# The rounded operand of the cross attention, made in the tokens' layout and transposed as bf16

## The chip, the cores and the metric

The kernel runs on one core of a Trainium2 chip. A core has five engines that run side by side and meet at semaphores: TensorE (PE in the profile, with its weight loads shown apart as PEld), VectorE (DVE), ScalarE (ACT), GpSimd (POOL) and SyncE (SP), which issues most of the DMAs. Work goes through the on-chip memory SBUF; TensorE writes into eight banks of PSUM. The metric is the device time of one execution in microseconds (us), here the median of three runs.

## The reference

One decoder layer on 4 batches of 512 tokens with 512 features. Three blocks, each behind its residual and followed by a layer normalisation without parameters: an attention-like mixer (`x1` is what comes out of it), a product with the context whose two operands are rounded to FP8, and an MLP with eight chosen experts for each token. Only the second block is touched by the change, together with the first units of the MLP that run beside it:

```python
def _fp8_quant_dequant(x):
    scale = 448.0 / jnp.maximum(jnp.max(jnp.abs(x)), 1e-12)
    q = jnp.clip(x * scale, -448.0, 448.0).astype(jnp.float8_e4m3fn)
    return q.astype(jnp.float32) / scale
out = jnp.einsum('bmk,bkn->bmn', _fp8_quant_dequant(x1), _fp8_quant_dequant(ctx_2048)) + mask
x2 = _layernorm(x1 + out)
mlp = silu(x2 @ gate_w) * (x2 @ up_w) @ down_w          # and the experts' sum is added
out = _layernorm(x2 + mlp + experts)
```

## The kernel before

A first phase computes `x1` for all four batches and leaves it in `xall`, 16 tiles of 128 tokens by 512 features, tokens along the partitions. The change lies in the start of the second phase (from line 1090; from about 212 us on).

**Rounding.** A tile of `x1` goes through four instructions. ScalarE scales it by `scale_x` into `y_q[i]` (L1420) and multiplies its magnitude by a constant into `m_q[i]` (L1422); VectorE adds and subtracts a number that size (L1547, L1549 in `quantise`), which leaves the value rounded to four bits, stored as bf16 in `x_q`. The product with the context (`cross`, L1879) needs features along the partitions, so TensorE first transposes the f32 tile with four 128x128 transposes (`transposes`, L1871) into a bank `gu`, and ScalarE's scaling reads that bank. All the rounding thus happens on transposed data, and `x_q` feeds `cross` directly.

**The units.** The MLP runs in units `n`: for one batch and 256 of the 2048 inner features, `gate_up` makes for each half `c` a gate product and an up product (12 matmuls 128x512 each, since every f32 operand is split into a high and a low part), ScalarE applies silu (`silu`, L1441), VectorE multiplies (`middle`, L1605), ScalarE and GpSimd split the result (`high_h` L1447, `low_h` L1302), and `down` or `down_early` multiplies it back into the banks `ob` (L1942 to L1946). Units 0 to 2 are interleaved with the second block: in unit `n` TensorE runs gate and up of half 0, then `cross(n + 1)`, then half 1, `down_early(n, 0)`, the transposes of the finished `x2` of batch n+1 (`x2_transposes`, L1862) and `down_early(n, 1)`. The transposes of `x1` for batch n+2 stand in units 0 and 1 in two groups of eight, one ahead of gate of half 1 and one between its gate and its up. Those of batch 1 stand at the very start, between the four tiles of `cross(0)`.

**VectorE beside it.** In unit `n` its queue holds `middle(n, 0)`, the residual of batch n+1 with its statistics (`residual`, L1557 and L1559), the variance (L1566), `quantise` of tile 0 of batch n+2, the normalisation (L1588), `middle(n, 1)`, `quantise` of tile 1, the low part of `x2` (L1594), two tiles of `accumulate` (L1614), `quantise` of tile 2, two more of `accumulate`, and `quantise` of tile 3. Every engine runs its queue strictly in this written order.

**GpSimd beside it.** It adds the mask to a batch of `xall` with a DMA that accumulates (`add_mask`, L152). That DMA changes `xall`, so it waits until the transposes of that batch have read it (`x1t_mm`). Behind it in the queue stands `power` (L1308), the inverse square root that the normalisation waits for, and then `low_h`.

Of the kernel before, what the change touches and what calls it, by code (L numbers as in the profile page):

```python
# [16 lines left out]
BF16 = mybir.dt.bfloat16  # L17
# [72 lines left out]
def decoder_layer(nc, x, ctx, mask, w_in, b_in, w_out, b_out, gamma, beta, w_q, keys, down_embed, up_embed,  # L90
# [14 lines left out]
    with ExitStack() as whole:  # L105
# [57 lines left out]
        with ExitStack() as first:  # L163
# [126 lines left out]
            def _(pool):  # L290
# [72 lines left out]
                add_mask(0)  # L363
# [726 lines left out]
        with ExitStack() as second:  # L1090
# [13 lines left out]
            junk2 = sb("junk2", [P, D], BF16)  # L1104
            key_sb = sb("key_sb", [P, 2, 2, NK], F32)
# [20 lines left out]
            late_junk = sb("late_junk", [P, D], BF16)  # L1126
# [32 lines left out]
            minus_first, squared = sem("minus_first"), sem("squared")  # L1159
            minus_done, squared_late, shift_done, y_act = sem("minus_done"), sem("squared_late"), sem("shift_done"), sem("y_act")  # L1160
# [5 lines left out]

            def x1t_bank(b, i):

                return i if b < 2 else i % 2

# [119 lines left out]
            def _(pool):  # L1290
# [42 lines left out]
                add_mask(1)  # L1333
# [66 lines left out]
            def _(act):  # L1400
# [12 lines left out]
                def scaled(b, tiles):  # L1413
                    for i in tiles:

                        j = TB * b + i
                        act.wait_ge(x1t_mm, j + 1)
                        if j >= TB:
                            act.wait_ge(q_done, j - TB + 1)
# [41 lines left out]
                scaled(0, range(TB))  # L1461
                scaled(1, (0, 1))
                for i in range(TB):
                    deviation(i)
                for n in range(TB - 1):
                    high_x2(n)
                    if n == 0:
                        scaled(1, (2, 3))
                        high_w(2, 0, 0, 2, 0)
                        high_w(3, 0, 0, 3, 1)  # L1470
                    unit(n, 0)
                    if n + 2 < TB:
                        scaled(n + 2, (0, 1))
                    silu(n, 1)
                    if n + 2 < TB:
                        scaled(n + 2, (2, 3))
# [58 lines left out]
            def _(dve):  # L1535
# [3 lines left out]
                def quantise(b, tiles):  # L1539
                    for i in tiles:  # L1540
# [309 lines left out]
            def _(pe):  # L1850
# [14 lines left out]
                def transposes(b, tiles, bank, count, free):  # L1865

                    for i in tiles:
                        free(i)
                        for c in range(KC):
                            j = TB * b + i  # L1870
                            last = nc.tensor.transpose(gu[bank(i)][:, c * P:(c + 1) * P], xall[:, j * D + c * P:j * D + (c + 1) * P], ident[:])  # L1871
                        last.then_inc(count, 1)
# [9 lines left out]
                def gate_up(n, g_set, tb, c, w_loads, between=None, up_free=None):  # L1882
# [5 lines left out]
                    if n < TB - 1 and c == 0:  # L1888
# [4 lines left out]
                        else:  # L1893
                            pe.wait_ge(y_done, TB + 2)
# [61 lines left out]
                def own_bank(i):  # L1956
                    return i

                def x1_bank(b):
                    return lambda i: x1t_bank(b, i)  # L1960

                def first_half_free(n):
                    return lambda i: pe.wait_ge(mid_done, GC * n + 1)
# [99 lines left out]
```

## Time and profile before

| | |
|---|---|
| median of 3 runs | 798.92 us (798.86 to 799.06) |
| the profiled execution's own time | 799.09 us |
| its span, first to last instruction | 797.2 us |
| TensorE busy | 778.9 us, 98% of the span |
| VectorE busy | 669.1 us, 84% |
| GpSimd busy | 368.5 us, 46% |
| ScalarE busy | 320.3 us, 40% |

A busy time is the sum over the records of an engine. Matmuls overlap in their pipeline: a 128x512 matmul is recorded as 0.39 us long, and the next one starts about 0.23 us behind it, so costs on TensorE are read from start to start. "[0.39 <-POOL h_lo L1302]" behind a row of the timeline means that the engine stood idle for 0.39 us ahead of it and that this instruction ended the wait. Some matmul records are missing from a trace, so that a row x15 can stand for 16.

### The profile page before, as it was taken

The numbers are of one execution on the slowest core, as the hardware profiler recorded it, in microseconds if no ns is written. First come the engines' busy times: TensorE is split into PE (matmuls) and PEld (weight loads), VectorE is DVE, ScalarE is ACT, GpSimd is POOL, SyncE is SP. The second block draws the span as 40 slices with busy tenths as digits, with TensorE's granted clock in tenths as the row PEclk, the third lists the DMA queues.
The fourth block names the chain that finished last, engine by engine and source line by source line (L and its number), as shares of the span: only waits on it lengthen the run. The fifth ranks groups of instructions, "written<-read, shape, count | busy, mean of one in ns | idle before, by whom it ended". The sixth has DMA issues, their size and how long they took to land. (4 is left out here: it accounts for less than half of the span.)

```text
span 797.2 us, 10711 instructions
## 1 busy us (share of the span) xinstructions
PE 778.9 (98%) x3610; PEld 639.3 (80%) x3614; DVE 669.1 (84%) x1330; ACT 320.3 (40%) x704; POOL 368.5 (46%) x305
## 2 busy tenths in 40 slices
PE   8999999999899999999999999999999999999996
PEld 7888888888667878888888888888877877878785
DVE  6887679898889870566699999999999999999997
ACT  6444337366574412232534323334233333333324
POOL 1331222233123411024467767676766667766433
PEclk9999999999999999999999999999999999999999
DMA  8667505625454538001222322322333233232113
GB/s 317 237 143 175 106 2 127 162 80 91 84 132 119 146 104 266 1 1 34 69 59 84 91 80 73 95 78 58 95 94 95 90 93 112 64 91 68 44 53 158
DMA packets 51046, 81.16 MB, mean 102 GB/s; under 512 B 17487, under 2 KB 26447, under 8 KB 50480
## 3 DMA queue, kind: packets, MB, share of 16 engines
q0 software_dynamic: 24240, 32.96, 19.4%
q1 hardware_dynamic: 25168, 47.52, 17.1%
q8 instruction: 28, 0.46, 0.2%
q10 hardware_dynamic: 1584, 0.01, 0.1%
q14 instruction: 26, 0.21, 0.1%
HBM read 110.44 MB, written 12.58 MB: 154 GB/s over the span
## 5 line engine op out<-in xcount | busy, mean ns | idle before, releaser
L1852 PE MATMUL gu<-x_hi,w_hi 128*128 128x512 f32 x516 | 202.1, 392 | 1.9 <-ACT mid L1441 1.9
L1854 PE MATMUL gu<-x_hi,w_lo 128*128 128x512 f32 x516 | 200.9, 389 | 0.0
L1853 PE MATMUL gu<-x_lo,w_hi 128*128 128x512 f32 x516 | 200.8, 389 | 0.0
L1302 POOL TENSOR_TENSOR h_lo<-mid,h_hi 128x512 fp32r<-128x512 f32 x62 | 80.6, 1320 | 103.5 <-ACT h_hi L1447 103.0
L1457 ACT ACTIVATE gates<-dots 128x1 f32<-128x1 f32 x144 | 29.2, 203 | 232.4 <-DVE dots L1696 226.4
L1852 PEld LDWEIGHTS gu<-x_hi,w_hi 128*128 128x128 f32 x516 | 96.9, 188 | 24.3 <-ACT mid L1441 4.4
L1854 PEld LDWEIGHTS gu<-x_hi,w_lo 128*128 128x128 f32 x516 | 96.8, 188 | 20.3
L1853 PEld LDWEIGHTS gu<-x_lo,w_hi 128*128 128x128 f32 x516 | 96.9, 188 | 19.8
L1321 POOL DMA_INDIRECT ctx_q<-table_dram,row_i x64 | 80.4, 1257 | 62.2 <-DVE xall L1705 42.5
L1321 POOL DMA_INDIRECT scratch<-table_dram,row_i x64 | 82.5, 1289 | 39.8 <-issue 23.6
L1605 DVE TENSOR_TENSOR mid<-gu,mid 128x512 f32<-128x512 f32 x64 | 44.2, 690 | 62.3 <-PE gu L1854 41.1
L1926 PE MATMUL ob<-w_lo,h_hi 128*128 128x512 f32 x224 | 87.2, 389 | 0.0
L1925 PE MATMUL ob<-w_hi,h_hi 128*128 128x512 f32 x224 | 87.2, 389 | 0.0
L1696 DVE CUSTOM_DVE_ANT_0 junk<-x_tok,scratch 128x512 bf16<-128x512 f32 x64 | 80.5, 1257 | 0.3
L1930 PE MATMUL ob<-w_hi,h_lo 128*128 128x512 f32 x224 | 69.2, 390 | 0.8 <-POOL h_lo L1302 0.8
L1696 DVE CUSTOM_DVE_ANT_0 junk<-x_tok,ctx_q 128x512 bf16<-128x512 f32 x64 | 66.0, 1032 | 0.5
L1297 POOL TENSOR_TENSOR w_lo<-xhat,w_hi 128x1024 fp32r<-128x1024 f32 x21 | 50.7, 2415 | 23.8 <-ACT w_hi L1411 15.9
L1768 DVE TENSOR_TENSOR xall<-ob,xall 128x512 f32<-128x512 f32 x95 | 59.6, 683 | 2.3 <-PE ob L1930 0.3
L1447 ACT ACTIVATE h_hi<-mid 128x512 fp32r<-128x512 f32 x62 | 36.0, 620 | 58.3 <-PE ob L1930 31.8
L1441 ACT ACTIVATE mid<-gu 128x512 f32<-128x512 f32 x64 | 37.2, 583 | 42.2 <-PE gu L1854 33.6
L1930 PEld LDWEIGHTS ob<-w_hi,h_lo 128*128 128x128 f32 x224 | 41.8, 188 | 10.2 <-POOL h_lo L1302 1.6
L1925 PEld LDWEIGHTS ob<-w_hi,h_hi 128*128 128x128 f32 x224 | 42.0, 188 | 8.8
(258 smaller groups left out, 1449.9 us busy)
## 6 DMA issues: line engine op xcount, KB each, us to landing
stage<-in_ctx SPq DMA_DIRECT2D x7, 1024.0 KB, 6.0
total<-prod POOLq DMA_DIRECT2D x11, 512.0 KB, 4.7
xall<-half_bo POOLq DMA_DIRECT2D x4, 1024.0 KB, 9.9
xhat<-in_L_ffn_gate_w SPq DMA_DIRECT2D x8, 512.0 KB
xhat<-in_L_ffn_up_w SPq DMA_DIRECT2D x8, 512.0 KB
xall<-in_mask_Bx1xS_ff POOLq DMA_DIRECT2D x4, 1024.0 KB, 10.5
xhat<-in_L_ffn_down_w SPq DMA_DIRECT2D x8, 512.0 KB
x_dram<-xall SPq DMA_DIRECT2D x4, 1024.0 KB, 7.0
```

Of the source, the lines that this page charges most:

```text
L1297: nc.gpsimd.tensor_tensor(flat(lo, r), stage_of(r, slot), flat(hi, r).bitcast(F32), ALU.subtract).then_inc(wlo_done, 1)
L1302: nc.gpsimd.tensor_tensor(lo[:, c], mid[c][:], hi[:, c].bitcast(F32), ALU.subtract).then_inc(hlo_done, 1)
L1321: nc.gpsimd.indirect_dma_start(rows[k], None, table_dram[:, :], bass.IndirectOffsetOnAxis(ap=row_i[t % 2][:, k:k + 1], axis=0), bounds_che ...
L1605: nc.vector.tensor_tensor(mid[c][:], gu[2 * c + 1][:], mid[c][:], ALU.mult).then_inc(mid_done, 1)
L1696: nc.vector.tensor_tensor_reduce(out=junk2[:], in0=x2_tok[par][:], in1=row[:, 0:D], scale=1.0, scalar=0.0, op0=ALU.mult, op1=ALU.add, accu ...
L1768: nc.vector.tensor_tensor(tile(j), ob[i][:], tile(j), ALU.add).then_inc(acc_done, 1)
L1852: nc.tensor.matmul(dst, lhs[0], rhs[0], start=start, stop=False)
L1853: nc.tensor.matmul(dst, lhs[0], rhs[1], start=False, stop=False)
L1854: return nc.tensor.matmul(dst, lhs[1], rhs[0], start=False, stop=stop)
L1925: nc.tensor.matmul(ob[i][:], h[0][:, c, ts], w_high[:, c], start=(c == 0), stop=False)
L1926: nc.tensor.matmul(ob[i][:], h[0][:, c, ts], w_low[:, c], start=False, stop=False)
L1930: last = nc.tensor.matmul(ob[i][:], h[1][:, c, ts], w_high[:, c], start=False, stop=(c == GC - 1))
```

## The change

For batches 1 to 3 the rounding works on `xall` itself, in the tokens' layout. ScalarE's scaling reads the tile in SBUF, `quantise` writes the rounded tile as bf16 into new tiles `x_qt[i]`, TensorE transposes those (`xq_transposes`, with a bf16 identity that GpSimd makes) into the banks `ob`, read as bf16, and ScalarE copies each bank to `x_q` (`copy_xq`). `cross` then waits for the copies. Batch 0 stays as it was. The sixteen transposes of a batch now stand in unit 0 behind up of half 0, and in units 1 and 2 between gate and up of half 0. ScalarE's instructions of a batch are grouped: four scalings at once and, after the silu of half 1, four magnitudes at once. `add_mask` of batches 1 to 3 waits for the scalings. At the start, where batch 1 was transposed, five transposes of the identity stand ahead of each of tiles 1 to 3.

```diff
@@ add_mask
-        def add_mask(b):
-            nc.gpsimd.wait_ge(x1t_mm, TB * (b + 1))
+        def add_mask(b, read, count):
+            nc.gpsimd.wait_ge(read, count)
@@ GpSimd
                 nc.gpsimd.memset(key_sb[:], 0.0).then_inc(key_zero, 1)
+                nc.gpsimd.tensor_copy(ident_b[:], ident[:]).then_inc(ident_b_done, 1)
...
-                        add_mask(n + 2)
+                        add_mask(n + 2, y_scaled, TB * (n + 3))
@@ ScalarE
-                def scaled(b, tiles):
...
-                        nc.scalar.activation(y_q[i], gu[x1t_bank(b, i)][:], ACT.Copy, scale=scale_x[:, 0:1]).then_inc(y_scaled, 1)
-                        act.wait_ge(y_scaled, j + 1)
-                        nc.scalar.activation(m_q[i], y_q[i], ACT.Abs, scale=ROUND_TO_4_BITS).then_inc(y_done, 1)
+                def scaled(b, i):
+                    j = TB * b + i
+                    if b:
+                        act.wait_ge(q_done, j - TB + 1)
+                    else:
                         act.wait_ge(x1t_mm, j + 1)
+                    nc.scalar.activation(y_q[i], tile(j) if b else gu[i][:], ACT.Copy, scale=scale_x[:, 0:1]).then_inc(y_scaled, 1)
+
+                def magnitude(b, i):
+                    j = TB * b + i
+                    act.wait_ge(y_scaled, j + 1)
+                    nc.scalar.activation(m_q[i], y_q[i], ACT.Abs, scale=ROUND_TO_4_BITS).then_inc(y_done, 1)
+
+                def copy_xq(b):
+                    for i in range(TB):
+                        act.wait_ge(xq_mm, TB * (b - 1) + i + 1)
+                        if i == 0:
+                            act.wait_ge(cross_mm, TB * b)
+                        nc.scalar.activation(x_q[:, i].rearrange("p c n -> p (c n)"), ob[i][:].bitcast(BF16)[:, 0:D], ACT.Copy).then_inc(xq_done, 1)
@@ VectorE, quantise
-                        if b and i == 0:
-                            dve.wait_ge(cross_mm, TB * b)
+                        if b > 1:
+                            dve.wait_ge(xq_mm, j - 2 * TB + 1)
...
-                        nc.vector.scalar_tensor_tensor(x_q[:, i].rearrange("p c n -> p (c n)"), m, ROUND_SUBNORMAL, y, ALU.max, ALU.subtract).then_inc(q_done, 1)
+                        nc.vector.scalar_tensor_tensor(x_qt[i][:] if b else x_q[:, i].rearrange("p c n -> p (c n)"), m, ROUND_SUBNORMAL, y, ALU.max, ALU.subtract).then_inc(q_done, 1)
@@ TensorE
+                def xq_transposes(b, free):
+                    for i in range(TB):
                         free(i)
+                        pe.wait_ge(q_done, TB * b + i + 1)
                         for c in range(KC):
+                            last = nc.tensor.transpose(ob[i][:].bitcast(BF16)[:, c * P:(c + 1) * P], x_qt[i][:, c * P:(c + 1) * P], ident_b[:])
+                        last.then_inc(xq_mm, 1)
...
                 def cross(b, free, tiles=range(TB)):
                     for i in tiles:
                         free(i)
-                        pe.wait_ge(q_done, TB * b + i + 1)
+                        if b:
+                            pe.wait_ge(xq_done, TB * (b - 1) + i + 1)
+                        else:
+                            pe.wait_ge(q_done, i + 1)
...
                 for n in range(TB - 1):
-                    gate_up(n, 0, n, 0, 2 if n == 0 else None)
-                    cross(n + 1, freed(acc_done, TB * (n - 1)) if n else nothing)
-                    if n + 2 < TB:
-                        transposes(n + 2, (0, 1), x1_bank(n + 2), x1t_mm, first_half_free(n))
-                        gate_up(n, 0, n, 1, None, lambda: transposes(n + 2, (2, 3), x1_bank(n + 2), x1t_mm, freed(y_done, TB * (n + 2) - 2)))
-                    else:
-                        gate_up(n, 0, n, 1, None)
+                    def next_xq():
+                        xq_transposes(n + 1, freed(acc_done, TB * (n - 1)) if n else nothing)
+                    gate_up(n, 0, n, 0, 2 if n == 0 else None, next_xq if n else None)
+                    if n == 0:
+                        next_xq()
+                    cross(n + 1, nothing)
+                    gate_up(n, 0, n, 1, None)
                     down_early(n, 0, freed(z2_done, TB * n))
                     x2_transposes(n + 1, x2_bank_free(n))
                     down_early(n, 1, nothing)
```

On TensorE in unit 1, at the end of gate of half 0, with bank numbers: before, the first products of up follow the last of gate.

```order
L1900 MATMUL gu0<-x2_lo,w_hi 128x512 [waits l2_done]
L1900 MATMUL gu0<-x2_lo,w_hi 128x512 x3
L1852 MATMUL gu1<-x2_hi,w_hi 128x512
L1853 MATMUL gu1<-x2_lo,w_hi 128x512
L1854 MATMUL gu1<-x2_hi,w_lo 128x512
```

Now the sixteen transposes of batch 2 stand there, each tile behind its `q_done`.

```order
L1919 MATMUL gu0<-x2_lo,w_hi 128x512 [waits l2_done]
L1919 MATMUL gu0<-x2_lo,w_hi 128x512 x3
L1889 MATMUL ob0<-ident_b,x_qt0 128x128 [waits q_done,acc_done]
L1889 MATMUL ob0<-ident_b,x_qt0 128x128 x3
L1889 MATMUL ob1<-ident_b,x_qt1 128x128 [waits q_done,acc_done]
L1889 MATMUL ob1<-ident_b,x_qt1 128x128 x3
L1889 MATMUL ob2<-ident_b,x_qt2 128x128 [waits q_done,acc_done]
L1889 MATMUL ob2<-ident_b,x_qt2 128x128 x3
L1889 MATMUL ob3<-ident_b,x_qt3 128x128 [waits q_done,acc_done]
L1889 MATMUL ob3<-ident_b,x_qt3 128x128 x3
L1870 MATMUL gu1<-x2_hi,w_hi 128x512
```

The transposes moved from either side of gate of half 1 to the front of up of half 0, and took with them a wait for the rounded tiles.

On ScalarE in unit 1, before: silu and high part of half 0, and the eight instructions of batch 3 around the silu of half 1 (L1420 scales, L1422 takes the magnitude).

```order
L1441 ACTIVATE mid0<-gu0 128x512 [waits hlo_done,gate_mm]
L1447 ACTIVATE h_hi<-mid0 128x512 [waits down_mm,mid_done]
L1420 ACTIVATE scratch<-gu0,scale_x 128x512 [waits q_done,x1t_mm]
L1422 ACTIVATE scratch<-scratch 128x512 [waits y_scaled]
L1420 ACTIVATE scratch<-gu1,scale_x 128x512 [waits q_done,x1t_mm]
L1422 ACTIVATE scratch<-scratch 128x512 [waits y_scaled]
L1441 ACTIVATE mid1<-gu2 128x512 [waits hlo_done,gate_mm]
L1420 ACTIVATE scratch<-gu0,scale_x 128x512 [waits q_done,x1t_mm]
L1422 ACTIVATE x2_tok0<-scratch 128x512 [waits y_scaled]
```

The same place now (L1432 is the copy of `copy_xq`, L1425 the magnitude).

```order
L1451 ACTIVATE mid0<-gu0 128x512 [waits hlo_done,gate_mm]
L1432 ACTIVATE scratch<-ob0 128x512 [waits cross_mm,xq_mm]
L1432 ACTIVATE scratch<-ob1 128x512 [waits xq_mm]
L1432 ACTIVATE scratch<-ob2 128x512 [waits xq_mm]
L1432 ACTIVATE scratch<-ob3 128x512 [waits xq_mm]
L1457 ACTIVATE h_hi<-mid0 128x512 [waits down_mm,mid_done]
L1420 ACTIVATE scratch<-xall,scale_x 128x512 [waits q_done] x4
L1451 ACTIVATE mid1<-gu2 128x512 [waits hlo_done,gate_mm]
L1425 ACTIVATE scratch<-scratch 128x512 [waits y_scaled] x2
L1425 ACTIVATE x2_tok0<-scratch 128x512 [waits y_scaled] x2
```

Four copies came in between silu and high part of half 0, and all magnitudes of batch 3 moved behind the silu of half 1.

## Rows read from the trace of the kernel before

**Rows 1.** The page's first part: busy time, share of the span, instructions.
```profile
PE 778.9 (98%) x3610; PEld 639.3 (80%) x3614; DVE 669.1 (84%) x1330; ACT 320.3 (40%) x704; POOL 368.5 (46%) x305
```

**Rows 2.** Windows: busy us of each engine, then clock share, DMA share, GB/s.
```profile
280.00:300.00 20.00, 19.93 (x98) 15.40 (x98) 14.26 (x28) 4.01 (x8) 3.55 (x3) 1.00 0.41 118
300.00:340.00 40.00, 40.00 (x194) 33.74 (x193) 12.84 (x61) 10.24 (x18) 5.31 (x4) 1.00 0.39 126
600.00:700.00 100.00, 98.94 (x434) 80.72 (x433) 93.82 (x161) 36.27 (x109) 71.24 (x52) 1.00 0.33 95
```

**Rows 3.** Timeline of TensorE, unit 1: start, duration, what, idle before.
```profile
253.46 1.07 PE L1900 MATMUL gu<-x_lo,w_hi 128*128 128x512 f32 x4
254.37 0.39 PE L1852 MATMUL gu<-x_hi,w_hi 128*128 128x512 f32 x1
...
257.32 3.40 PE L1879 MATMUL ob<-ctx_q,scratch 128*128 128x512 bf16 x15
260.55 1.04 PE L1871 MATMUL gu<-ident,xall 128*128 128x128 f32 x8
261.35 0.47 PE L1852 MATMUL gu<-x_hi,w_hi 128*128 128x512 f32 x1
```

**Rows 4.** Groups by line: weight loads; busy us, mean ns | idle before.
```profile
L1879 PEld LDWEIGHTS ob<-ctx_q,scratch 128*128 128x128 bf16 x64 | 5.7, 98 | 8.1 <-DVE scratch L1549 1.1 <-issue 0.8
L1871 PEld LDWEIGHTS gu<-ident,xall 128*128 128x128 f32 x48 | 5.6, 140 | 1.4
```

**Rows 5.** Timeline of ScalarE: first deviation, copies out of PSUM, a magnitude, a silu.
```profile
220.14 0.72 ACT L1435 ACTIVATE junk<-xall,z_minus 128x512 bf16<-128x512 f32 x1 [0.21 <-DVE z_minus L1574]
...
248.25 2.04 ACT L1428 ACTIVATE x_hi<-gu 128x512 fp32r<-128x512 f32 x4
...
263.15 0.63 ACT L1422 ACTIVATE scratch<-scratch 128x512 bf16<-128x512 f32 x1
264.40 0.60 ACT L1441 ACTIVATE mid<-gu 128x512 f32<-128x512 f32 x1 [0.61 <-PE gu L1854]
```

**Rows 6.** Timeline of VectorE, unit 0: first residual and normalisation.
```profile
236.44 0.75 DVE L1557 SCALAR_TENSOR_TENSOR xall<-ob,unscale,xall 128x512 f32<-128x512 f32 x1 [0.98 <-DMA xall<-in_mask_Bx1xS_ff]
...
244.21 1.92 DVE L1588 TENSOR_SCALAR xall<-xall,mv,rstd 128x512 f32<-128x512 f32 x4 [0.20 <-POOL rstd L1308]
```

**Rows 7.** Timeline of TensorE, unit 0: its wait in `down_early(0, 1)`.
```profile
249.25 0.50 PE L1946 MATMUL ob<-w_hi,h_lo 128*128 128x512 f32 x1 [0.39 <-POOL h_lo L1302]
```

**Rows 8.** Timeline of VectorE: low part of x2, last rounding of batches 2 and 3.
```profile
248.86 2.48 DVE L1594 TENSOR_TENSOR x_lo<-gu,x_hi 128x512 fp32r<-128x512 f32 x4 [0.81 <-ACT x_hi L1428]
...
255.70 0.69 DVE L1549 SCALAR_TENSOR_TENSOR scratch<-x_tok,scratch 128x512 bf16<-128x512 bf16 x1
...
279.45 0.69 DVE L1549 SCALAR_TENSOR_TENSOR scratch<-x_tok,scratch 128x512 bf16<-128x512 bf16 x1
```

**Rows 9.** Timeline of VectorE, unit 1, from middle to the normalisation.
```profile
257.36 0.69 DVE L1605 TENSOR_TENSOR mid<-gu,mid 128x512 f32<-128x512 f32 x1 [0.36 <-PE gu L1854]
...
264.23 0.17 DVE L1566 TENSOR_SCALAR var<-mv 128x4 f32<-128x4 f32 x1
264.32 0.69 DVE L1547 SCALAR_TENSOR_TENSOR scratch<-scratch 128x512 f32<-128x512 bf16 x1
265.05 0.69 DVE L1549 SCALAR_TENSOR_TENSOR scratch<-scratch 128x512 bf16<-128x512 bf16 x1
267.97 1.92 DVE L1588 TENSOR_SCALAR xall<-xall,mv,rstd 128x512 f32<-128x512 f32 x4 [2.23 <-POOL rstd L1308]
```

**Rows 10.** Timeline of GpSimd, unit 1: the mask's DMA and the power.
```profile
265.54 1.33 POOL L152 DMA_DIRECT2D xall<-in_mask_Bx1xS_ff  x1 [4.87 <-PE gu L1871]
266.39 1.55 POOL L1308 TENSOR_TENSOR rstd<-var,neg_half 128x4 f32<-128x4 f32 x1
```

**Rows 11.** Timeline of TensorE, unit 2: first product of up, of gate of half 1.
```profile
278.14 0.39 PE L1852 MATMUL gu<-x_hi,w_hi 128*128 128x512 f32 x1
...
284.14 0.58 PE L1852 MATMUL gu<-x_hi,w_hi 128*128 128x512 f32 x1
```

More of the change, by code:

```diff
@@ L362, in _ @@
                 last_z_rstd(slice(0, TB))
-                add_mask(0)
+                add_mask(0, x1t_mm, TB)
                 for i in range(TB):
@@ L1104, in decoder_layer @@
             junk2 = sb("junk2", [P, D], BF16)
+            x_qt = [sb(f"x_qt{i}", [P, D], BF16) for i in range(TB)]
+            ident_b = sb("ident_b", [P, P], BF16)
             key_sb = sb("key_sb", [P, 2, 2, NK], F32)
@@ L1125, in decoder_layer @@
             late_square = sb("late_square", [P, TB + 1], F32)
-            late_junk = sb("late_junk", [P, D], BF16)
+            late_junk = x_qt[0]
             z_sum = sb("z_sum", [P, TB], F32)
@@ L1159, in decoder_layer @@
             minus_first, squared = sem("minus_first"), sem("squared")
+            ident_b_done, xq_mm, xq_done = sem("ident_b_done"), sem("xq_mm"), sem("xq_done")
             minus_done, squared_late, shift_done, y_act = sem("minus_done"), sem("squared_late"), sem("shift_done"), sem("y_act")
@@ L1165, in tile @@
                 return xall[:, bass.ds(j * D, D)]
-            def x1t_bank(b, i):
-                return i if b < 2 else i % 2
             def x2t_bank(b, i):
@@ L1330, in _ @@
                 nc.gpsimd.memset(key_sb[:], 0.0).then_inc(key_zero, 1)
+                nc.gpsimd.tensor_copy(ident_b[:], ident[:]).then_inc(ident_b_done, 1)
                 power_pair(0)
                 power_pair(1)
-                add_mask(1)
+                add_mask(1, y_scaled, 2 * TB)
                 for n in range(TB):
@@ L1459, in experts @@
                         nc.scalar.activation(coef[:, t % 2, k:k + 1], gates[:, t % 2, k:k + 1], ACT.Copy, scale=prob[:, t, k:k + 1]).then_inc(coef_done, 1)
-                scaled(0, range(TB))
-                scaled(1, (0, 1))
+                for i in range(TB):
+                    scaled(0, i)
+                    magnitude(0, i)
+                for i in range(TB):
+                    scaled(1, i)
                 for i in range(TB):
@@ L1467, in _ @@
                     if n == 0:
-                        scaled(1, (2, 3))
+                        for i in range(TB):
+                            magnitude(1, i)
                         high_w(2, 0, 0, 2, 0)
                         high_w(3, 0, 0, 3, 1)
-                    unit(n, 0)
+                    silu(n, 0)
+                    copy_xq(n + 1)
+                    high_h(n, 0)
                     if n + 2 < TB:
-                        scaled(n + 2, (0, 1))
+                        for i in range(TB):
+                            scaled(n + 2, i)
                     silu(n, 1)
                     if n + 2 < TB:
-                        scaled(n + 2, (2, 3))
+                        for i in range(TB):
+                            magnitude(n + 2, i)
                     high_h(n, 1)
@@ L1863, in x2_transposes @@
                         last.then_inc(x2t_mm, 1)
-                def transposes(b, tiles, bank, count, free):
-                    for i in tiles:
+                def xq_transposes(b, free):
+                    for i in range(TB):
                         free(i)
+                        pe.wait_ge(q_done, TB * b + i + 1)
                         for c in range(KC):
-                            j = TB * b + i
-                            last = nc.tensor.transpose(gu[bank(i)][:, c * P:(c + 1) * P], xall[:, j * D + c * P:j * D + (c + 1) * P], ident[:])
-                        last.then_inc(count, 1)
+                            last = nc.tensor.transpose(ob[i][:].bitcast(BF16)[:, c * P:(c + 1) * P], x_qt[i][:, c * P:(c + 1) * P], ident_b[:])
+                        last.then_inc(xq_mm, 1)
                 def cross(b, free, tiles=range(TB)):
@@ L1954, in nothing @@
                     pass
[L1956 to L1963, printed above, removed]
[L1965 to L1974 removed]
+                def x2_bank_free(n):
+                    return lambda i: pe.wait_ge(mid_done, GC * n + 1 + i // 2)
                 def keep_running(bank, count):
@@ L1983, in _ @@
                 keep_running(ob[3], 5)
-                for i in range(TB):
-                    transposes(1, (i,), own_bank, x1t_mm, freed(y_done, 0))
+                cross(0, nothing, (0,))
+                for i in range(1, TB):
+                    pe.wait_ge(y_done, i + 1)
+                    keep_running(gu[0], 5)
                     cross(0, nothing, (i,))
-                pe.wait_ge(y_done, TB + 2)
                 for i in range(1, TB):
```

15 lines of the change are left out of this document (1 added, 14 removed).

## The prediction, made before the changed kernel was run

> **What bounds the kernel now.** I read the page's shares first: TensorE is busy for 98% of the span [rows 1]. The windows say whether that holds at the place of the change: from 280 to 300 us it works 19.93 of 20 us, from 300 to 340 all of it, and from 600 to 700 us it idles for 1.06 [rows 2]. So what TensorE gets more to do, or waits longer for, in the first units moves all that comes behind. Its timeline gives the prices, from start to start. The up product of half 0 in unit 1 begins at 254.37, and the first recorded `cross` product, the second of 16, at 257.32; the first stood at 257.10, so 12 products take 2.73 us [rows 3]. `cross` runs from there to 260.55, 3.45 us, 0.216 each. Eight f32 transposes take 0.80 from start to start, and the product behind them is recorded 0.08 longer than the others, so 0.88, 0.11 each.
>
> **What is removed.** Units 0 and 1 lose two groups of eight f32 transposes each: 4 x 0.88 = 3.52 us of TensorE time in a stretch without slack. The sixteen of batch 1 at the start stood between waits for VectorE's rounding of batch 0, and fifteen transposes of the identity stand in their place: nothing.
>
> **What is added on TensorE.** 48 bf16 transposes, which no row shows. From below: a bf16 product of 512 columns takes 0.216, a quarter of that for 128 columns is 0.054. From above: the f32 transpose's 0.11. The bf16 weight load is recorded at 98 ns and that of the f32 transpose at 140 [rows 4]; I scale 0.11 by that, 0.08, so 1.28 us for a batch. By count alone the change comes out at 3.84 - 3.52 = +0.3 us, and between -0.9 and +1.8 at the two ends.
>
> The trace shows f32 transposes 0.11 us apart although each is recorded 0.27 long (eight in 1.04 us from the first start to the last end [rows 3]). The Trainium skill, "TensorE: Matmul & The Clock Gate", Part 4, puts a 128x128 bf16 transpose at about 275 ns in a kernel's context; if that were the step and not only the length, this sum would not hold, and the last rival below would be the forecast.
>
> **ScalarE's copies.** Four more instructions for each batch. The nearest row is the copy of `x2` out of PSUM, four in 2.04 us [rows 5], 0.51 each and 0.6 for a single one. In units 1 and 2 they lie beside the 2.73 us of up; in unit 0 the first lies open. The grouping costs ScalarE nothing in itself: in the start its fourth scaling of batch 1 follows the last rounding of batch 0 at once, and it idled for 0.21 before the first deviation at 220.14 [rows 5]. The small cast of the identity lies in GpSimd's idle start.
>
> **Unit 0.** TensorE finishes up, transposes tile 0 (0.32), waits for its copy (0.6 and two handovers of about 0.05) and starts `cross`; the other twelve transposes lie beside the copy for the most part. `cross` starts some 1.2 us later than before. Of half 1 both groups of transposes are gone, 1.76, so TensorE is 0.6 us early at the down products. That gain ends in a wait. The chain of VectorE in unit 0 begins with the landing of batch 1's mask at 236.44, whose DMA the change doesn't move, and leads over residual, variance and normalisation at 244.21 [rows 6] to `middle(0, 1)`, the high and the low part, and the product that waited for GpSimd until 249.25 [rows 7]. Only the 0.20 us for the power goes, since batch 2's mask is issued before the variance is there. I carry -0.18 us out of unit 0 (from -0.2 to +0.3).
>
> **Unit 1, where the new wait decides.** The fourth tile of batch 2 is rounded at 255.70 + 0.69 = 256.39 [rows 8]. VectorE works towards that without a gap from 248.86 on: the low part of `x2`, two accumulations, tile 2, two accumulations, tile 3. The change leaves this order. Before, that was in time, as `cross` needed the tile only at the end of up. Now its transposes stand ahead of up. TensorE comes to them at 254.37 - 0.18 + 12 x 0.08 = 255.15, the tile is there at 256.21: a wait of 1.06 us that nothing covers, since up stands behind it in the same queue. Up starts at 256.21 + 0.06 + 0.32 = 256.59 instead of 254.37, **+2.22 us**.
>
> What becomes of that: up (2.73) and `cross` (3.45) bring gate of half 1 to 262.77, against 261.35 [rows 3], +1.42, and without the second group TensorE is at the down products at +0.54. VectorE's middle at 257.36 and variance at 264.23 [rows 9] move by 2.22, to 266.45. But VectorE had waited 2.23 us for the power, which stood behind the mask's DMA, and that behind the transposes of tiles 2 and 3 for 4.87 us [rows 10]. Now the mask follows the four scalings, near 263.6, and the power follows the variance: 266.65 + 1.55 = 268.2. The rounding of batch 3's tile 0 stands ahead of the normalisation. It now waits for its magnitude, which stands behind silu: 264.40 + 1.42 + 0.60 + 0.63 [rows 5] gives 267.0, and 1.41 us of rounding [rows 9] lead to 268.4. So the normalisation starts at 268.4 instead of 267.97, and the delay **s** on VectorE's chain is 0.4 us. TensorE's product that waits for the low part follows it by the same 0.4 or 0.5. The mask gives back most of what unit 1's wait cost.
>
> **Unit 2, where it stays.** Batch 3's fourth tile is rounded at 279.45 + 0.69 + 0.4 = 280.54 [rows 8], and TensorE arrives at 278.14 + 0.45 + 0.96 = 279.55: again a wait of 1.0 us. Up starts at 280.54 + 0.06 + 0.32 = 280.92 instead of 278.14 [rows 11], **+2.78 us**. No transposes are removed here, as before none stood behind `cross` (gate of half 1 follows it at 284.14), and TensorE has no idle time up to 340 us [rows 2] in which it could vanish. VectorE's residuals move with it. Query products, routing and experts begin behind TensorE's units, so they move too.
>
> **The sum.** Unit 0 gives -0.18, unit 1 moves up by +2.22 with that in it, the chain carries +0.4 of it into unit 2, and unit 2's own wait and last four transposes add 2.4. At the end +2.8 us. Against the profiled execution's own 799.09 that is 801.9, against the median 798.92 it is 801.7. Its own range: s from 0 (power and magnitude in time) to 1.2 (slower low part, busier GpSimd), four transposes 0.22 to 0.44: +2.3 to +3.7, 801.2 to 802.6. About 0.2%, 1.6 us, is what a measurement of this kernel can tell from no change, so this case is slower by more than that.
>
> **Rivals.**
> - *The mask's earlier start wins.* For: a power that is 2 us earlier takes VectorE's 2.23 us of idle time away. If unit 1's wait did not come first, batch 3's last tile would be ready near 278.2 and only about +0.4 us would remain: 799.3, not slower. It decides by whether the fourth tile of batch 2 is rounded before 255.15. Against: that part of the chain hangs on the landing at 236.44, which stays. Chance 0.08.
> - *The count decides.* Bf16 transposes at 0.054 and no wait that is new: 48 x 0.054 - 3.52 = -0.9, and the waits for the low part, 0.39 [rows 7], partly gone: about 797.8. Against: the same 256.39. Chance 0.04.
> - *Absorbed later.* TensorE idles for about 1% between 600 and 700 us, so VectorE and GpSimd bound it there at times; if their chain did not start behind TensorE's units it would take the delay: 799.3. Against: the routing that starts it waits for TensorE. Chance 0.03.
> - *ScalarE and GpSimd get late too.* High part, scalings, silu and magnitudes stand behind four copies, so each hold-up there is passed on, to the power as well: 0.7 us more in each of units 1 and 2, 803.1. Chance 0.12.
> - *Transposes in steps of their recorded length.* At 0.27 each, sixteen take 4.3 us in front of up. Unit 1 comes to +4.2, of which 1.8 are saved behind it, and unit 2 adds 4.3 to 2.5: about +6.9, 805.8. This is the case of the skill's figure above. The f32 rows speak against it. Chance 0.02.
>
> **How the numbers follow.** The forecast has 0.71. Slower by over 0.2%: 0.71 + 0.12 + 0.02 = 0.85. Within 0.2%: 0.08 + 0.03 and a quarter of the count's case, 0.12. Faster: 0.03. The range from 800.6 to 803.2 takes in the forecast's own range with a margin, and the case of the late ScalarE; it leaves out about 0.17 for the others.
>
> **What would show it.** In the timeline of TensorE of the changed kernel: idle time of about 1 us in the middle of the new transposes of units 1 and 2, ended by VectorE's rounding; up starting near 256.6 and 280.9; steps of about 0.08 between bf16 transposes; the waits for `h_lo` in units 0 and 1 still there. On VectorE: no 2.23 us wait for the power, a short one for ScalarE instead, the normalisation near 268.4. I am wrong if TensorE passes the new transposes without waiting, if the copies hold up `cross` in units 1 and 2, or if the delay at 300 us isn't the one at the end.

## The result: 801.87 us, 0.36% slower, with the two waits where they were expected

| | before | after |
|---|---|---|
| median | 799.03 us (798.77 to 799.27) | 801.87 us (801.69 to 802.18) |
| ratio of after to before | | 1.0036 (1.0024 to 1.0048) |
| the profiled execution's own time | 799.09 us | 802.12 us |
| its span | 797.2 us | 800.3 us |

Both medians are of seven executions on one chip. The forecast was 801.7, with a range from 800.6 to 803.2. The page's first part hardly differs: TensorE's 778.9 us of busy time are those of [rows 1] to the last digit, and ScalarE has 5.3 us more with twelve more instructions, the copies.

```profile
PE 778.9 (97%) x3629; PEld 638.4 (80%) x3629; DVE 668.7 (84%) x1330; ACT 325.6 (41%) x716; POOL 368.0 (46%) x306
```

The span has grown by 3.1 us and the busy time by nothing, so TensorE waits longer. The list of TensorE's waits (engine, tile and line, what ended the wait: us in total, times, longest) says for what, in its first line:

```profile
PE ob L1889 <- DVE x_qt L1567: 2.7, 2, 1.3
```

L1889 is the new transpose, L1567 the last instruction of `quantise`. The timeline of TensorE of the changed kernel shows the place of each. L1900 is now `cross`, L1916 and L1919 the gate, L1870 to L1872 the up products, L1961 to L1965 `down_early`.

```profile
228.09 0.47 PE L1916 MATMUL gu<-x_hi,w_hi 128*128 128x512 f32 x1 [0.45 <-ACT x_hi L1438]
...
233.64 1.12 PE L1889 MATMUL ob<-ident_b,x_qt 128*128 128x128 bf16 x16
234.73 3.63 PE L1900 MATMUL ob<-ctx_q,scratch 128*128 128x512 bf16 x16
...
249.81 0.50 PE L1965 MATMUL ob<-w_hi,h_lo 128*128 128x512 f32 x1 [0.89 <-POOL h_lo L1301]
...
254.93 0.84 PE L1889 MATMUL ob<-ident_b,x_qt 128*128 128x128 bf16 x12
257.11 0.38 PE L1889 MATMUL ob<-ident_b,x_qt 128*128 128x128 bf16 x4 [1.34 <-DVE x_qt L1567]
257.30 0.48 PE L1870 MATMUL gu<-x_hi,w_hi 128*128 128x512 f32 x1
...
279.18 0.84 PE L1889 MATMUL ob<-ident_b,x_qt 128*128 128x128 bf16 x12
281.35 0.38 PE L1889 MATMUL ob<-ident_b,x_qt 128*128 128x128 bf16 x4 [1.32 <-DVE x_qt L1567]
281.54 0.48 PE L1870 MATMUL gu<-x_hi,w_hi 128*128 128x512 f32 x1
...
287.66 0.58 PE L1870 MATMUL gu<-x_hi,w_hi 128*128 128x512 f32 x1
...
792.51 0.61 PE L1949 MATMUL ob<-w_hi,w_lo 128*128 128x512 f32 x2
```

In units 1 and 2 three tiles are transposed, then TensorE stands idle for 1.34 and 1.32 us until the fourth is rounded, and up of half 0 stands behind that. VectorE and GpSimd beside it, from their timelines in the changed kernel (L1575 residual, L1584 variance, L1565 and L1567 rounding, L1606 normalisation, L1623 middle, L1307 power):

```profile
237.01 0.75 DVE L1575 SCALAR_TENSOR_TENSOR xall<-ob,unscale,xall 128x512 f32<-128x512 f32 x1 [0.97 <-DMA xall<-in_mask_Bx1xS_ff]
...
244.78 1.92 DVE L1606 TENSOR_SCALAR xall<-xall,mv,rstd 128x512 f32<-128x512 f32 x4 [0.20 <-POOL rstd L1307]
...
256.27 0.69 DVE L1567 SCALAR_TENSOR_TENSOR x_qt<-x_tok,scratch 128x512 bf16<-128x512 bf16 x1
...
260.41 0.69 DVE L1623 TENSOR_TENSOR mid<-gu,mid 128x512 f32<-128x512 f32 x1 [2.84 <-PE gu L1872]
...
267.29 0.17 DVE L1584 TENSOR_SCALAR var<-mv 128x4 f32<-128x4 f32 x1
267.70 0.69 DVE L1565 SCALAR_TENSOR_TENSOR scratch<-scratch 128x512 f32<-128x512 bf16 x1 [0.24 <-ACT scratch L1425]
268.43 0.69 DVE L1567 SCALAR_TENSOR_TENSOR x_qt<-scratch 128x512 bf16<-128x512 bf16 x1
269.04 1.91 DVE L1606 TENSOR_SCALAR xall<-xall,mv,rstd 128x512 f32<-128x512 f32 x4
```

```profile
243.34 1.41 POOL L1307 TENSOR_TENSOR rstd<-var,neg_half 128x4 f32<-128x4 f32 x1 [2.64 <-DVE var L1584]
...
264.52 1.33 POOL L152 DMA_DIRECT2D xall<-in_mask_Bx1xS_ff  x1 [1.40 <-ACT scratch L1420]
267.55 1.03 POOL L1307 TENSOR_TENSOR rstd<-var,neg_half 128x4 f32<-128x4 f32 x1 [1.70 <-DVE var L1584]
```

Against [rows 9] and [rows 10]: the mask goes out 1.0 us earlier although everything ahead of it is 2.9 us later, the wait for the power in front of the normalisation (2.23 us) is gone, and a short one for ScalarE's magnitude (0.24) stands ahead of the rounding. VectorE's idle time has moved to the front of `middle`, where it waits for up: 2.84 us instead of 0.36.

**An offset of this execution.** Everything is 0.57 us late before unit 1 comes: the mask of batch 1 is issued at 225.41 instead of 224.84, and the residual follows at 237.01 instead of 236.44 [rows 6]. About 0.16 of it stands already at 209 us, ahead of the changed code, where the transposes of L1077 start at 209.27 instead of 209.11. For the rest, 0.41 us, the windows of the start (after; us busy by engine, granted clock, DMA share, GB/s) show the granted clock at 0.50, the lower of TensorE's two levels, 1.2 GHz:

```profile
215.00:217.00 2.00, 1.53 (x6) 0.83 (x7) 1.97 (x4) 1.94 (x5) 0.00 (x0) 0.73 0.25 52
217.00:219.00 2.00, 2.00 (x8) 1.21 (x7) 1.93 (x4) 2.00 (x4) 0.00 (x0) 0.50 1.01 338
219.00:221.00 2.00, 2.00 (x13) 1.36 (x12) 1.93 (x7) 1.86 (x4) 0.00 (x0) 0.92 0.08 22
```

The kernel before shows 1.00 in the same windows. What TensorE did before the fall can be read from its timeline: five transposes of the identity at 213.28, an idle time of 1.42 us, then `cross(0)` from 215.47. I come back to it with the third experiment.

### The profile page after: what moved, and what is told of

Read it like the earlier page. It is cut to its first block and busy times, and to the rows that moved or that the text cites. A ratio compares the mean times of both kernels' runs of the same rounds, so it can differ in the third digit from the quotient of the medians.

```text
span 800.3 us, 10753 instructions
## 1 busy us (share of the span) xinstructions
PE 778.9 (97%) x3629; PEld 638.4 (80%) x3629; DVE 668.7 (84%) x1330; ACT 325.6 (41%) x716; POOL 368.0 (46%) x306
## 5 line engine op out<-in xcount | busy, mean ns | idle before, releaser
L1870 PE MATMUL gu<-x_hi,w_hi 128*128 128x512 f32 x516 | 202.4, 392 | 1.5 <-ACT mid L1451 1.4
L1872 PE MATMUL gu<-x_hi,w_lo 128*128 128x512 f32 x516 | 200.9, 389 | 0.0
L1870 PEld LDWEIGHTS gu<-x_hi,w_hi 128*128 128x128 f32 x516 | 96.9, 188 | 24.1 <-ACT mid L1451 4.1
L1872 PEld LDWEIGHTS gu<-x_hi,w_lo 128*128 128x128 f32 x516 | 96.9, 188 | 20.2
L1623 DVE TENSOR_TENSOR mid<-gu,mid 128x512 f32<-128x512 f32 x64 | 44.2, 690 | 67.3 <-PE gu L1872 46.1
L1945 PEld LDWEIGHTS ob<-w_lo,h_hi 128*128 128x128 f32 x224 | 42.1, 188 | 8.8
```

The costliest lines, as they stand in the source:

```text
L1623: nc.vector.tensor_tensor(mid[c][:], gu[2 * c + 1][:], mid[c][:], ALU.mult).then_inc(mid_done, 1)
L1870: nc.tensor.matmul(dst, lhs[0], rhs[0], start=start, stop=False)
L1872: return nc.tensor.matmul(dst, lhs[1], rhs[0], start=False, stop=stop)
L1945: nc.tensor.matmul(ob[i][:], h[0][:, c, ts], w_low[:, c], start=False, stop=False)
```

## The experiments

The theory: TensorE's wait for the fourth tile, ahead of up, makes the change slower, and the earlier mask keeps the two waits from adding up. The rivals: the transposes themselves or the copies cost it; the mask's new wait is not what gives time back; the start does it. The starts of four instructions in the profiled execution of each kernel, and the medians (us; 5 to 11 executions each; before was measured twice beside them, with 22 and 27 executions; the ratio of after is that of its own comparison, above):

| kernel | up, unit 1 | normalisation, unit 1 | up, unit 2 | last product | median | ratio to before |
|---|---|---|---|---|---|---|
| before | 254.37 | 267.97 | 278.14 | 789.37 | 799.11, 799.07 | |
| after | 257.30 | 269.04 | 281.54 | 792.51 | 801.87 | 1.0036 |
| fourth tile behind up | 255.17 | 267.15 | 277.96 | 789.34 | 799.02 | 1.0004 (0.9995 to 1.0013) |
| all tiles behind up | 254.50 | 267.21 | 277.36 | 789.39 | 799.44 | 1.0002 (0.9993 to 1.0011) |
| start filled | 256.75 | 268.49 | 281.00 | 792.12 | 801.69 | 1.0034 (1.0022 to 1.0047) |
| mask late | 257.63 | 270.74 | 283.25 | 794.17 | 804.09 | 1.0062 (1.0048 to 1.0076) |
| before, with the wait | 256.50 | 270.24 | 282.47 | 793.61 | 805.15 | 1.0079 (1.0065 to 1.0093) |
| before, mask first | 253.90 | 267.50 | 277.66 | 788.82 | 798.40 | 0.9991 (0.9982 to 1.0) |
| all repairs | 253.97 | 265.89 | 276.71 | 788.00 | 797.44 | 0.9980 (0.9971 to 0.9989) |
| tile 0 ahead of up | 253.78 | 265.70 | 276.54 | 787.78 | 797.56 | 0.9982 (0.9973 to 0.9991) |

### The wait alone taken away: the fourth tile behind up

```diff
-                    gate_up(n, 0, n, 0, 2 if n == 0 else None, next_xq if n else None)
-                    if n == 0:
-                        next_xq()
+                    gate_up(n, 0, n, 0, 2 if n == 0 else None, (lambda: next_xq((0, 1, 2))) if n else None)
+                    next_xq((3,) if n else range(TB))
```

> The changed kernel with one thing moved: in units 1 and 2 only the transposes of tiles 0 to 2 stand between gate and up, those of tile 3, which wait for VectorE's last rounding, stand behind up. Theory (TensorE's two new waits of 1.34 and 1.32 us decide): no idle time in the new transposes, up of unit 1 near 255.8 instead of 257.3, cross of unit 1 starts 1.35 earlier, VectorE's normalisation of unit 1 near 267.8 instead of 269.0, up of unit 2 near 278.7 instead of 281.5; the end 2.3 to 2.6 us earlier than the changed kernel, 799.2 to 799.6 us. Rival (the work itself, 48 bf16 transposes and 12 copies, is what costs): the end moves by 0.3 us at most, 801.5. Rival (tile 3's copy, now open behind up, holds up cross): TensorE idles for about 0.6 us ahead of its last four cross products in units 1 and 2, 800.5.

Timeline of TensorE of this kernel:

```profile
254.52 0.84 PE L1889 MATMUL ob<-ident_b,x_qt 128*128 128x128 bf16 x12
255.17 0.48 PE L1870 MATMUL gu<-x_hi,w_hi 128*128 128x512 f32 x1
...
258.01 0.40 PE L1889 MATMUL ob<-ident_b,x_qt 128*128 128x128 bf16 x4
258.46 3.40 PE L1900 MATMUL ob<-ctx_q,scratch 128*128 128x512 bf16 x15
...
277.31 0.84 PE L1889 MATMUL ob<-ident_b,x_qt 128*128 128x128 bf16 x12
277.96 0.48 PE L1870 MATMUL gu<-x_hi,w_hi 128*128 128x512 f32 x1
```

No idle time ahead of up in either unit, the normalisation 1.89 us earlier than in the changed kernel (0.42 of it is offset: the first residual of unit 0 is at 236.59 here, at 237.01 there), and with eight transposes out of 48 moved, four in each of two units, the whole loss is gone: 799.02 us. So neither the transposes nor the copies nor the start make the change slow; the place of one tile's transposes does. The rows also give the price that no row of before had: twelve transposes take 0.65 us from the first to the product behind them, **0.054 us each**. That was the lower bound of my sum (a quarter of a `cross` product), not the 0.08 that I took.

### No transposes ahead of up at all

```diff
-                    gate_up(n, 0, n, 0, 2 if n == 0 else None, next_xq if n else None)
-                    if n == 0:
-                        next_xq()
+                    gate_up(n, 0, n, 0, 2 if n == 0 else None)
+                    next_xq()
```

> The changed kernel with the sixteen transposes of units 1 and 2 behind up, as in unit 0. Theory (the wait for the last rounding decides; the copies need no cover, as TensorE transposes for 1.1 us while the first is made): the same as with tile 3 alone behind up, 799.2 to 799.6 us, and cross follows the sixteenth transpose without idle time. Rival (the copies need up as their cover): TensorE idles for 0.5 to 1.0 us ahead of cross in units 1 and 2, 800.0 to 801.0 us.

Here all four copies lie open between the transposes and `cross`. Timeline of TensorE:

```profile
257.22 1.07 PE L1889 MATMUL ob<-ident_b,x_qt 128*128 128x128 bf16 x16
258.54 3.40 PE L1900 MATMUL ob<-ctx_q,scratch 128*128 128x512 bf16 x15 [0.25 <-ACT scratch L1432]
```

`cross` waits for the first copy for about 0.24 us: sixteen steps of 0.054 end at 258.08, and the first `cross` product, whose record is missing, stood one step of 0.216 ahead of 258.54, at 258.32. It never waits for the others, since each is copied while the tile before it is multiplied. Unit 2 shows the same row with the same 0.25. So ScalarE's copies need next to no cover, and the last product at 789.39 is where the kernel before has it, 789.37. The medians of this kernel and the one above differ by 0.4 us, less than either scatters. Part of that scatter lies behind the last product: the profiled execution here took 800.40 us with a span of 798.6, so 9.2 us follow that product instead of the 7.8 of the kernel before. The places on the timeline compare these kernels better than single times do.

### The start filled

```diff
-                keep_running(ob[3], 5)
+                keep_running(ob[3], 12)
```

> The changed kernel with twelve instead of five transposes of the identity ahead of the first cross product, so that TensorE idles for about 0.6 us there instead of 1.42. Theory (the granted clock of 0.50 from 217 to 219 us of the changed kernel's trace followed that idle time and cost 0.45 us at the first gate): clock 1.00 in that stretch, the first gate product about 0.45 us earlier against the first phase's end, the end about 0.4 us earlier, 801.4 us. Rival (the low clock is not tied to the longer idle time, or the time is made up by 1 core's later waits): no change within 0.1 us, 801.9.

Twelve instead of five transposes of the identity stand ahead of the first tile of `cross(0)`, in idle time. The windows of this kernel:

```profile
215.00:217.00 2.00, 1.66 (x11) 1.22 (x13) 1.95 (x4) 1.94 (x4) 0.00 (x0) 1.00 0.38 119
217.00:219.00 2.00, 2.00 (x14) 1.37 (x13) 1.94 (x4) 2.00 (x4) 0.00 (x0) 1.00 0.86 291
```

The clock stays up, gate begins at 227.32 instead of 228.09, and up of unit 2 at 281.00. Of the 0.77 us at gate, 0.35 stand already at 209 us. The first residual of unit 0 starts at 236.45, against 236.44 [rows 6], so that profiled execution is the changed kernel without its offset, and by it my positions can be read best: 256.75 measured for 256.59 forecast, 281.00 for 280.92, 2.75 us at the last product for 2.8. The median falls by 0.18 us only, which is inside the scatter of both; I had expected 0.4. A likely reason is that the low clock does not come in every execution: the mean granted clock of the changed kernel's seven executions is 0.995 in the profiled one and 0.997 to 0.999 in the six others. In the kernel with all tiles behind up, five transposes and an idle time of 1.65 us stand ahead of `cross(0)`, more than the 1.42 of the changed kernel, and its windows show no fall:

```profile
215.00:217.00 2.00, 1.55 (x10) 1.19 (x12) 1.97 (x4) 1.94 (x4) 0.00 (x0) 1.00 0.35 69
217.00:219.00 2.00, 2.00 (x14) 1.29 (x12) 1.93 (x4) 2.00 (x4) 0.00 (x0) 1.00 0.98 340
```

The kernels with the fourth tile behind up and with the late mask have it (0.57 and 0.50 in the lowest window). From the transposes at 209 us to the issue of the first mask it is 16.14 us in the changed kernel and in that with the fourth tile behind up, and 15.73 in the kernel before, in that with the start filled and in that with all tiles behind up: the low clock costs 0.41 us there. With the late mask it is 15.81, so a fall need not cost that much. What decides whether the clock falls is open: with twelve transposes ahead of the first tile it held in all three profiled executions that have them (here and in the two kernels at the end), with five it held in one and fell in three.

### The mask held back

```diff
-                        add_mask(n + 2, y_scaled, TB * (n + 3))
+                        add_mask(n + 2, y_done, TB * (n + 2) + 1)
```

The mask of batches 2 and 3 waits for the first magnitude again, which stands behind silu of half 1, about as late as the transposes of before.

> The changed kernel with the mask of batches 2 and 3 waiting for the first magnitude of the batch (behind the silu of half 1, about where the wait for TensorE's transposes had put it) instead of the scalings. Theory (the earlier mask lets the power follow the variance and so gives back over 1 us of unit 1's delay): the mask's DMA of unit 1 is issued near 267.7 instead of 264.5, the power near 269.0, the normalisation near 270.4 instead of 269.04, up of unit 2 1.3 us later, the end 803.1 to 803.3 us. Rival (the mask's place decides nothing, as VectorE waits for the magnitude anyway): 801.9.

Timelines of GpSimd and of VectorE of this kernel:

```profile
268.31 1.33 POOL L152 DMA_DIRECT2D xall<-in_mask_Bx1xS_ff  x1 [4.85 <-ACT scratch L1425]
269.15 1.55 POOL L1307 TENSOR_TENSOR rstd<-var,neg_half 128x4 f32<-128x4 f32 x1
```

```profile
245.11 1.92 DVE L1606 TENSOR_SCALAR xall<-xall,mv,rstd 128x512 f32<-128x512 f32 x4 [0.92 <-POOL rstd L1307]
...
270.74 1.92 DVE L1606 TENSOR_SCALAR xall<-xall,mv,rstd 128x512 f32<-128x512 f32 x4 [1.28 <-POOL rstd L1307]
```

Compared with [rows 10], power stands right behind the mask again, and the normalisation 1.70 us later than in the changed kernel. The median is 2.2 us above that of the changed kernel, where 1.2 to 1.4 had been expected. The first of these VectorE rows says why: unit 0's normalisation waits 0.92 us for the power instead of 0.20. I had costed the late mask for unit 1 alone. At the last product the two profiled executions are only 1.66 us apart, but the changed kernel's carries its offset of 0.57 at the first residual and this one 0.18; against the start filled it is 2.05 us. So the mask's new wait is worth 2.0 to 2.2 us, and without it the change would have been 0.62% slower.

### The wait alone, put into the kernel before

```diff
-                    gate_up(n, 0, n, 0, 2 if n == 0 else None)
+                    gate_up(n, 0, n, 0, 2 if n == 0 else None, (lambda: pe.wait_ge(q_done, TB * (n + 2))) if n else None)
```

Nothing else of the change is in this kernel: between gate and up of half 0, TensorE waits for the rounded tiles that `cross` needs anyway.

> The kernel before with nothing added but the wait: in units 1 and 2 TensorE waits between gate and up of half 0 until VectorE has rounded all four tiles of the next batch. Theory (the wait in front of up is the cost, and the old place of the mask passes all of it on): idle 2.0 us ahead of up in unit 1 (rounding done at 256.4, gate at 254.4), the mask and the power 2.1 us later, VectorE's normalisation near 270.0 instead of 267.97, up of unit 2 near 282.3 instead of 278.1, the end about 4.1 us later than before, 803.2 us. Rival (VectorE's idle time takes unit 1's delay up even without an earlier mask): only unit 2's own 2.1 us stay, 801.2 us.

Timeline of TensorE:

```profile
256.50 0.50 PE L1852 MATMUL gu<-x_hi,w_hi 128*128 128x512 f32 x1 [1.90 <-DVE scratch L1549]
...
282.47 0.50 PE L1852 MATMUL gu<-x_hi,w_hi 128*128 128x512 f32 x1 [1.92 <-DVE scratch L1549]
```

Two waits of 1.9 us, not covered by any transposes, and both stay: with the mask still behind the transposes the normalisation is at 270.24 and waits its 2.23 us for the power, so nothing of unit 1's wait is given back. The last product is 4.2 us later. The profiled execution's own time, 803.31 us, is what was expected; the median of the five, 805.15, is not. They spread from 803.31 to 806.41, and mean granted clocks of 0.998, 0.998, 0.995, 0.993 and 0.993 go along with the times in this order. A profile exists only of the first, so where the other 2 to 3 us lie is open; the size of this run is taken from the profiled execution alone.

### One line in the kernel before: the first mask ahead of the powers

```diff
+                add_mask(1)
                 power_pair(0)
                 power_pair(1)
-                add_mask(1)
```

> The kernel before with one line moved: batch 1's mask ahead of GpSimd's two first powers. Theory: the first residual 0.9 us earlier, the wait of 0.39 us for the low part in unit 0 gone, in unit 1 VectorE still waits for the power behind the mask of batch 3: 0.4 to 0.7 us less than before, 798.5. Rival (nothing waits for that chain but for 0.39 us, which unit 1's wait for the mask takes back): 799.1.

The mask of batch 1 is issued at 219.68 instead of 224.84, the first residual of unit 0 starts at 235.20 without the wait for the DMA of [rows 6], and the product that had waited for `h_lo` starts at 248.78 with no wait marked, against 249.25 [rows 7]. The timeline of VectorE shows where most of the 1.24 us is caught again:

```profile
243.74 1.92 DVE L1588 TENSOR_SCALAR xall<-xall,mv,rstd 128x512 f32<-128x512 f32 x4 [0.98 <-POOL rstd L1308]
```

The next mask now stands ahead of a power that VectorE waits for. Half a microsecond remains, 788.82 at the last product, 798.40 us (with a ratio whose interval just reaches 1): the chain of unit 0 did begin at the mask's landing, as the forecast said.

### All repairs, and tile 0 earlier

The first of these two kernels takes the change and adds to it: the fourth tile behind up, twelve transposes of the identity in the start, batch 1's mask ahead of the powers, and ScalarE's magnitude of tile 0 ahead of the silu of half 1:

```diff
+                add_mask(1, y_scaled, 2 * TB)
...
-                add_mask(1, y_scaled, 2 * TB)
...
+                        magnitude(n + 2, 0)
                         silu(n, 1)
-                        for i in range(TB):
+                        for i in range(1, TB):
```

> The changed kernel with tile 3's transposes behind up in units 1 and 2, twelve products of the identity at the start, the magnitude of tile 0 ahead of the silu of half 1, and batch 1's mask ahead of GpSimd's two first powers (it then waits for the scalings only). Theory (unit 0 is bound by the landing of batch 1's mask): the first residual starts near 235.5 instead of 236.5, TensorE's wait for the low part in unit 0 falls from 0.9 to about 0.1 us, and all behind it is 0.8 to 0.9 us earlier than with tile 3 alone behind up: 798.0 to 798.3 us. Rival (unit 0 is not bound there, or the gain is lost at VectorE in units 1 and 2): 799.0.

```profile
265.89 1.92 DVE L1607 TENSOR_SCALAR xall<-xall,mv,rstd 128x512 f32<-128x512 f32 x4 [0.21 <-POOL rstd L1307]
```

797.44 us, 1.6 us under before and 4.4 under the changed kernel, and 0.6 below the lower end of what was expected. In this row of VectorE the normalisation waits 0.21 us for a power that follows its variance directly, and no longer for ScalarE. Against the kernel with only the fourth tile moved, the first residual is 1.23 us earlier (235.36 instead of 236.59), the normalisation of unit 1 1.26 and the last product 1.34: with the later masks out of the way of the powers, what the first mask gains is not caught again, as it was in the kernel before. The earlier magnitude gives almost nothing: from the aggregation of the statistics to the normalisation it is 2.13 us here and 2.18 there, since the power lasted 1.42 us here and 1.03 there. No run separates the parts further.

The second also puts tile 0's transposes of unit 0 ahead of up, so that its copy is hidden.

> As with all repairs, and in unit 0 tile 0's transposes stand between gate and up and the other twelve behind up. Theory (the 0.20 us that TensorE idles ahead of cross in unit 0 is the latency of the first copy): this idle time goes and, unit 0 being bound by TensorE now, the end is 0.1 to 0.3 us earlier than with all repairs, 797.8 to 798.1. Rival (VectorE's chain binds unit 0 still): no difference.

```profile
233.19 0.84 PE L1890 MATMUL ob<-ident_b,x_qt 128*128 128x128 bf16 x12
233.87 3.62 PE L1901 MATMUL ob<-ctx_q,scratch 128*128 128x512 bf16 x16
```

`cross` follows twelve transposes with nothing between, and the last product is 0.22 us earlier, but the medians are 797.56 and 797.44: no difference that these runs can tell.

## Why the prediction was right, step by step

**The two waits, and why both count.** Right in place and releaser, and near in size: 1.34 and 1.32 us for a forecast of 1.06 and 1.0. They are longer because the twelve transposes ahead of them are shorter, 0.65 us instead of 0.96; a wait for VectorE takes up what TensorE saves in front of it. From the end of the rounding (256.96) to up it is 0.34, forecast 0.38. Free of the offset, up of unit 1 moves by 257.30 - 254.93 = 2.37 us (forecast 2.40), that of unit 2 by 3.40 - 0.57 = 2.83 (2.78). The first and the fifth experiment show the cause from both sides: without the wait the loss is gone, and with nothing but the wait it is there.

**The price of a transpose.** The one term that was mis-sized: 0.054 us each, not 0.08. By count alone the change is 48 x 0.054 - 3.52 = -0.9 us, not +0.3. It didn't reach the sum, as the time saved fell ahead of waits: the one just named, and in unit 0 the one for `h_lo`, which grew from 0.39 to 0.89 us. So the forecast came out well without this term being right, and its agreement says nothing for it. Scaling by the recorded weight loads pointed the wrong way. The groups by line of the changed kernel give 220 ns for each new transpose and 97 for its weight load, against a step of 54:

```profile
L1889 PE MATMUL ob<-ident_b,x_qt 128*128 128x128 bf16 x48 | 3.6, 220 | 2.7 <-DVE x_qt L1567 2.7
L1889 PEld LDWEIGHTS ob<-ident_b,x_qt 128*128 128x128 bf16 x48 | 2.7, 97 | 3.8 <-issue 3.7
```

The 275 ns that the Trainium skill, "TensorE: Matmul & The Clock Gate", Part 4, gives for a bf16 transpose in a kernel's context is of the order of such a record's length and five times the step; the rival of steps as long as the records, 805.8, fell.

**Unit 0.** The small failure. I gave the change -0.18 us for a power that no longer stands behind the mask. The normalisation still waits 0.20 us for it. GpSimd's timeline of the kernel before tells why:

```profile
242.88 1.30 POOL L1308 TENSOR_TENSOR rstd<-var,neg_half 128x4 f32<-128x4 f32 x1
```

The variance there ended at 242.78, so this power followed it at once and the mask had not held it up; the 0.20 is what a power of 1.3 us lasts beyond VectorE's rounding of one tile. The forecast took unit 0's wait for the same case as unit 1's [rows 10], without a row for it.

**Normalisation of unit 1, s = 0.4.** Forecast 268.4. Measured 269.04, less the offset 268.47; with the filled start 268.49. Power and magnitude were both nearly in time, as worked out; the power lasted 1.03 us instead of the 1.55 taken, which did not count, as the rounding ended last.

**Behind unit 2.** Nothing noticeable is absorbed: from up of unit 2 to the last product it is 511.23 us before, 510.97 after, and between 510.92 and 511.38 in the kernels of the table but one. With all tiles behind up it is 512.03, as there sixteen transposes (0.86) and the wait for the copy (0.24) stand behind up. At most a tenth of a delay is lost on the way, 0.3 us here.

**The sum.** +2.84 us between the medians, for a forecast of +2.8. In the profiled execution the last product is 3.14 us later, 0.57 of it the offset; the remaining 2.57 are 2.83 at up of unit 2 less the 0.3 lost behind it. That the forecast did not foresee an offset and that this one does not come in every execution leaves the agreement of the medians good to some 0.3 us and no better.

**The rivals.** *The mask wins*: the first experiment is its case, with up of unit 1 free of the wait, and gave 799.02 for a forecast of 799.3; the mechanism is real, but the wait comes first. *The count decides* needed that as well, and even with it the shorter transposes brought nothing: what unit 0 saves goes mostly into its wait for `h_lo`, and what unit 1 saves is what the sixteen transposes of unit 2 take. *Absorbed later* fell by the nearly constant 511 us. *ScalarE gets late* fell: it came 0.24 us late at one place.

**The signs.** All that were named came, but for two: the step of 0.08 was 0.054, and of the waits for `h_lo` only unit 0's is in the list of waits; in unit 1 that product starts 0.29 us behind the one ahead of it, where it was 0.50 before and the usual step is 0.23.

## What to carry to other kernels

Work moved to another place on an in-order engine brings its waits along, and everything that stood behind the new place now waits too: before placing it, write down when its last input is ready on the other engine, and put behind the next covered block whatever is not ready by then, tile by tile and not the group as a whole. Two changes on one chain (a later product, an earlier DMA) don't add up: of the 1.24 us by which the first residual came earlier with one mask moved, half a microsecond was left, since the next mask stood in front of the power. For short matmuls read the step from start to start up to the next instruction; the recorded length says little of it.

## What the runs showed that I had not expected

A bf16 transpose of 128x128 costs TensorE 0.054 us in a row of them, just the quarter of a 512-column bf16 product (0.216) that its columns make, though it is recorded with 220 ns and its weight load with 97; the f32 one takes 0.11 [rows 3]. The granted clock fell to half for some 3 us in the start of three kernels (idle times of 1.42, 1.68 and 1.82 us ahead of `cross(0)`) and stayed whole in another with 1.65 us at the same place, so the idle time alone doesn't tell it. GpSimd's power took 1.01 to 2.04 us for the same 128x4 elements, the longest in the kernel with the late mask, at 243.03 right behind a DMA issue.
